# Float32r operands against pairs of float16 under powers of two, with transposing transfers that write the operand of p v, in a one-core attention and FFN block

## The reference

```
x = x + attn(layernorm(x))
    q = x wq, k = x wk, v = x wv                 (wq's first 128 of 192 columns of each head)
    probs = softmax(causal(q k^T * 192**-0.5))
    attn = concat_heads(probs v) wo
x = x + ffn(layernorm(x))
    h = relu(s0 * x W0) * 2 ; h = relu(s1 * scaled(h) W1) * 2 ; s2 * scaled(h) W2     (W: +1 or -1 from booleans)
```

## Time and profile before

| | |
|---|---|
| median of 3 executions | 1190.53 us (1190.52 to 1191.59) |
| the profiled execution's own time | 1192.84 us |
| its span, first to last instruction | 1191.0 us |
| PE busy | 1153.1 us, 97% |
| PE weight loads | 1007.5 us, 85% |
| ACT, DVE, POOL busy | 842.5, 835.0, 740.2 us |
| granted TensorE clock, mean | 0.987 |

### The profile page before, as it was taken

The page is one execution under the profiler, slowest core; times in us unless marked ns, Lnnn a source line. Parts: engine busy times, 40 slices in busy tenths (PEclk is TensorE's granted clock), DMA queues, the critical chain, the costliest instruction groups (busy, mean ns, idle before and its releaser), DMA issues.

```text
span 1191.0 us, 21994 instructions
## 1 busy us (share of the span) xinstructions
PE 1153.1 (97%) x6214; PEld 1007.5 (85%) x6214; DVE 835.0 (70%) x1560; ACT 842.5 (71%) x1447; POOL 740.2 (62%) x709
## 2 busy tenths in 40 slices
PE   6689999999999999999999999999999999999798
PEld 5578988888888988888898888888898888888577
DVE  6667676667777676677777776777767667677673
ACT  4477777777777776777777776777777677777653
POOL 2557666767757677677757676676766666773210
PEclk9889999999999999999999999999999999999899
DMA  4055553544455544444545454454554354444501
GB/s 133 14 107 109 109 109 82 119 94 86 97 108 110 109 100 90 98 107 88 106 103 112 91 110 95 82 115 93 108 110 103 84 117 99 86 107 74 109 1 71
DMA packets 354552, 114.36 MB, mean 96 GB/s; under 512 B 305888, under 2 KB 348384, under 8 KB 354528
## 3 DMA queue, kind: packets, MB, share of 16 engines
q1 hardware_dynamic: 354528, 114.08, 45.5%
HBM read 36.44 MB, written 2.10 MB: 32 GB/s over the span
## 4 chain that ended last, share of the span: by engine, by line
PE 94%; DVE 2%; issue 1%; ACT 1%; DMA 1%; POOL 0%; SPq 0%; DVEq 0%; ACTq 0%; POOLq 0%
PE psC L1012 59%; PE psS L1012 17%; PE psC L1137 17%; PE psS L1023 1%; DMA res<-in_L_attn_hidden_states 0%; DVE xn L803 0%; DMA pt<-p 0%; DVE psS L881 0%; ACT psS L656 0%; DVE res L904 0%; DVE p L889 0%; DVE xb L829 0%; POOL wqk L461 0%; ACT xb L627 0%; ACT p L668 0%
## 5 line engine op out<-in xcount | busy, mean ns | idle before, releaser
L1012 PE MATMUL psC<-xb,wqk 128*128 128x512 f32 x1350 | 343.6, 393 | 2.6 <-DVE xb L809 1.5
L881 DVE CUSTOM_DVE_ANT_0 psS<-psS,mask 128x128 f32<-128x128 f32 (+7 forms) x256 | 194.7, 766 | 161.9 <-PE psS L1012 161.9
L678 ACT ACTIVATE pT<-pt 128x256 fp32r<-128x256 f16 (+7 forms) x256 | 293.6, 1159 | 15.1 <-DMA pt<-p 14.9
L1012 PEld LDWEIGHTS psC<-xb,wqk 128*128 128x128 f32 x1350 | 249.2, 189 | 50.2 <-issue 3.5
L1012 PE MATMUL psS<-qkT 128*128 128x512 f32 (+2 forms) x1152 | 252.5, 347 | 12.5 <-DVE p L889 9.9
L656 ACT ACTIVATE psS<-psS,negmax 128x128 f32<-128x128 f32 (+7 forms) x256 | 182.9, 715 | 108.8 <-DVE negmax L881 106.7
L510 POOL TENSOR_TENSOR qkT<-qk,qkT 128x512 fp32r<-128x512 f32 x124 | 159.3, 1295 | 152.3 <-ACT qkT L647 152.3
L1012 PEld LDWEIGHTS psS<-qkT 128*128 128x128 f32 x1152 | 202.4, 192 | 43.1 <-DVE p L889 11.2
L1012 PE MATMUL psC<-wos,attn 128*128 128x512 f32 x768 | 217.2, 396 | 7.4 <-DVE attn L871 6.6
L1137 PE MATMUL psC<-pT,v 128*128 128x512 f32 (+2 forms) x1152 | 221.1, 346 | 0.0
L1137 PEld LDWEIGHTS psC<-pT,v 128*128 128x128 f32 x1152 | 196.6, 188 | 28.5 <-issue 0.4
(11 more groups left out here) (85 smaller groups left out, 870.8 us busy)
## 6 DMA issues: line engine op xcount, KB each, us to landing
raw<-in_L_attn_wkv SPq DMA_DIRECT2D x64, 256.0 KB, 3.7
raw<-in_L_attn_wq SPq DMA_DIRECT2D x32, 256.0 KB, 3.1
raw<-in_L_attn_wo SPq DMA_DIRECT2D x32, 256.0 KB, 2.8
pt<-p SPq DMA_TRANSPOSE x256, 3.4
res<-in_L_attn_hidden_states SPq DMA_DIRECT2D x8, 256.0 KB, 5.7
out<-res SPq DMA_DIRECT2D x8, 256.0 KB, 2.0
raw<-in_L_ffn_k SPq DMA_DIRECT2D x3, 256.0 KB, 3.7
scl<-in_L_ffn_s SPq DMA_DIRECT2D x3, 0.5 KB, 4.7
```

The source lines that it names most:

```text
L678: nc.scalar.activation(pT[:, :, places_of(n), :], src, ACT.Copy, scale=1.0 / UP).then_inc(placed, 1)
L881: nc.vector.tensor_tensor_reduce(row, row, mask[:, S - width:S], -SCALE, 3e38, ALU.add, ALU.min, negmax[:, n:n + 1]).then_inc(max_done, 1)
L1012: last = nc.tensor.matmul(out_ap, w, x, start=k == 0, stop=k == len(terms) - 1)
```

## The change

It does five things.

1. xb, wqk, wvs, qkT, v and pT become float16. A LO or HI of a weight or of x is then a float16. The layer norm's scale is multiplied by 2^9 (`X_UP`), and each head's q and k weights, and each pair's v weights, by a power of two that is made on the chip: ACT sums the squares of the rows of the loaded weights (`row_squares`, step `mx`), SP writes the 128 sums to DRAM (`put`) and reads them back to all partitions (`get`), DVE adds them up and takes the exponent by bit operations (`bounds`, step `sc`: five small instructions, four for v), and ACT multiplies the weights in place (`scale_weights`, step `r`). The scale comes off again in work that is there anyway: `OUT_DOWN` in the activations' scale and in what were tensor_tensor and are now scalar_tensor_tensor on DVE, `undo_qk` in the maxima, `undo_v` (step `rv`) at p v. The third split of the v weights takes one addition on POOL where it took two.
2. `h` and `l` write p16 with HI and LO blocks in turn, and the transposing transfer writes pT itself. `place` and the block of zeros are gone, and pT has a half for each parity of the head.
3. No stream is widened: scores of block 0 have 128 columns, block 4 is 512 and 128, the last diagonal block of p v is 128.
4. wo, attn and the FFN stay float32r; the FFN has its own buffers, and POOL's three waits for buffers before the FFN's weights go.
5. The orders, the preamble and the banks are new. The startup loads the first head's weights ahead of x and runs mx, put, get, sc and r before the first split.

The diff, cut to its core:

```diff
 TENSOR_ORDERS = ("""
-    pv1@-1 s3@0 v0@0 s4@0 v1@0 s5@0 x3@1 v2@0 x4@1 v3@0 s6@0 x5@1 o4@-1 s7@0 x6@1 o5@-1 x7@1 o6@-1 pv0@0 v4@0 o7@-1
-    s0@1 v5@0 s1@1 v6@0 o0@0 v7@0 o1@0 s2@1 o2@0 s3@1 o3@0 pv1@0 s4@1 x1@2 s5@1 x2@2 o4@0 x3@2 s6@1 x4@2 s7@1 x5@2
-    x6@2 o5@0 x7@2 o6@0 pv0@1 o7@0 x1@3 s0@2 x2@3 o0@1 o1@1 s1@2 o2@1 s2@2 o3@1""", """
+    pv1@-1 s2@0 v0@0 s3@0 v1@0 x1@1 s4@0 o4@-1 s5@0 v2@0 x2@1 v3@0 s6@0 x3@1 s7@0 x4@1 o5@-1 x5@1 o6@-1 x6@1 o7@-1
+    x7@1 v4@0 pv0@0 v5@0 s0@1 v6@0 o0@0 s1@1 v7@0 o1@0 s2@1 o2@0 s3@1 o3@0 pv1@0 s4@1 s5@1 x1@2 o4@0 x2@2 o5@0 s6@1
+    o6@0 x3@2 s7@1 x4@2 o7@0 x5@2 pv0@1 x6@2 x7@2 o0@1 o1@1 o2@1 o3@1 s0@2 s1@2""", """
...
 SCALAR_ORDERS = ("""
-    h5@-1 c3@-1 qk0@0 e6@-1 h6@-1 c4@-1 e7@-1 c5@-1 h7@-1 qk2@0 qk3@0 c6@-1 pv0@-1 qk1@0 snap0@1 e0@0 h0@0 c7@-1
...
+    e7@-1 h7@-1 pv0@-1 qk3@0 qk2@0 r0@1 e0@0 h0@0 e1@0 qk1@0 h1@0 mx0@2 pv1@-1 e2@0 v0@0 h2@0 e3@0 h3@0 v1@0 snap0@1
...
 SYNC_ORDERS = ("""
-    t7@-1 t0@0 t1@0 t2@0 lqk0@2 lo0@0 t3@0 t4@0 t5@0 t6@0 lv0@2 t7@0 t0@1 t1@1 t2@1 lo0@1 t3@1 t4@1 lqk0@3 lv1@2
-    t5@1 t6@1""", """
+    t1@-1 put0@1 t2@-1 t3@-1 get0@1 t4@-1 t5@-1 lqk0@2 t6@-1 t7@-1 t0@0 t1@0 t2@0 put0@2 t3@0 lo0@0 lqk0@3 t4@0
+    get0@2 lv0@2 t5@0 t6@0 put1@2 lo0@1 t7@0 get1@2 t0@1""", """
...
-        xb = sb("xb", [P, 7, 2, 2, CH], F32R)
-        v = sb("v", [P, 2, NT, GH * DN], F32R)
-        pT = sb("pT", [P, 2, PLACES, P], F32R)
+        v = sb("v", [P, 2, NT, GH * DN], F16)
...
+            def rows_to_dram(g, j, n):
...
+                    wait(sp, rows_max[0], g, 1, j, 1)
...
+                sp.dma_start(wmax_dram[at:at + 1, :].rearrange("a p -> p a"), wmax[:, at:at + 1]) \
+                    .then_inc(rows_out[n], 16)
...
+                sp.dma_start(wrow[:, at, :], wmax_dram[at, :].partition_broadcast(P)).then_inc(rows_in[n], 16)
...
-                            wait(sp, placed, g, 8, j, n - 1)
-                            sp.sem_inc(turn_go, 1)
-                        sp.dma_start_transpose(turned_blocks(n), p16[:, n % 2, 0:2 * (n + 1) * P]) \
+                        sp.dma_start_transpose(pT[:, j % 2, rows_of(n), :], p16[:, n % 2, 0:2 * (n + 1) * P]) \
                             .then_inc(turned[n % 2], 16)
...
+                nc.scalar.activation(src, src, ACT.Copy, scale=bound[:, at, 3:4]).then_inc(scaled[n], 1)
...
+                nc.scalar.activation(squares[:, :], src.rearrange("p a s -> p (a s)"), ACT.Square,
+                                     accum_out=wmax[:, at:at + 1]).then_inc(rows_max[n], 1)
...
-            def place(g, j, n):
-
...
-                src = turned_blocks(n).rearrange("p (w k) s -> p w k s", w=2)
-                nc.scalar.activation(pT[:, :, places_of(n), :], src, ACT.Copy, scale=1.0 / UP).then_inc(placed, 1)
...
-                nc.vector.tensor_tensor(to, product, base32, ALU.add).then_inc(gathered[n], 1)
+                nc.vector.scalar_tensor_tensor(to, product, OUT_DOWN, base32, ALU.mult, ALU.add).then_inc(gathered[n], 1)
...
+                width = (n + 1) * P
+                for a, b in [(0, min(width, CH)), (CH, width)][:1 + n // 4]:
...
-                wait(pe, placed, g, 8, j, 4 * c + 4)
+                for n in range(2):
+                    wait(pe, turned[n], g, 64, j, 32 * c + 32)
...
-                    o = psC[:, bank, (4 - max(n, 2)) * P:]
+                    n = 4 * c + 4 - i
+                    o = psC[:, bank, (i - 4 * c) * P:CH]
```

More of the change, by code:

```diff
@@ L12 @@
 U8 = mybir.dt.uint8
+U32 = mybir.dt.uint32
 P = 128
@@ L95, in exists @@
     h = GH * g + step[1]
-    if h == 0 and (step[0] in ("x", "a", "snap", "sum", "qk") or step[0] == "wv" and step[2] == 2):
+    if h == 0 and (step[0] in ("x", "a", "snap", "sum", "qk", "mx", "sc", "r", "put", "get", "lqk", "lv") or step[0] == "wv" and step[2] == 2):
         return False
@@ new lines, in load_values @@
+            def load_values(pair):
+                for c in range(2):
+                    sp.dma_start(raw[:, 5 + c, :].rearrange("p (c e) -> p c e", c=2),
+                                 wv_v[:, 2 * c:2 * c + 2, bass.ds(pair, 1), :].rearrange("p c a e -> p c (a e)")) \
+                        .then_inc(loaded["v"], 16)
+            def rows_to_dram(g, j, n):
+                at = 2 if n else j % 2
+                if n:
+                    wait_pair(sp, rows_max[1], g, 1, j, 1)
+                    sp.sem_inc(turn_go, 1)
+                    wait_pair(sp, rows_in[1], g, 16, j, 0)
+                else:
+                    wait(sp, rows_max[0], g, 1, j, 1)
+                    sp.sem_inc(turn_go, 1)
+                    wait(sp, rows_in[0], g, 16, j, -16)
+                sp.dma_start(wmax_dram[at:at + 1, :].rearrange("a p -> p a"), wmax[:, at:at + 1]) \
+                    .then_inc(rows_out[n], 16)
@@ L411, in sync_steps @@
                 for step, j, n in steps_of(SYNC_ORDERS, g):
-                    if isinstance(g, int) and GH * g + j == 0 and step in ("lqk", "lv"):
+                    if isinstance(g, int) and GH * g + j == 0 and step in ("lqk", "lv", "put", "get"):
                         continue
@@ L515, in split_out @@
                 wait(pool, done["o"], g, 8, j, 0)
-                split(raw[:, 2, :], wos[:, HI, :], wos[:, LO, :], wo_hi, wo_lo, lambda: wait(pool, wo_hi, g, 1, j, 1))
+                nc.gpsimd.tensor_tensor(wos[:, HI, :], raw[:, 4, :], one[:, :].to_broadcast([P, D]), ALU.mult) \
+                    .then_inc(wo_hi, 1)
+                wait(pool, wo_hi, g, 1, j, 1)
+                nc.gpsimd.tensor_tensor(wos[:, LO, :], raw[:, 4, :], wos[:, HI, :].bitcast(F32), ALU.subtract) \
+                    .then_inc(wo_lo, 1)
             def split_values(g, j, n):
@@ L650, in exponentials @@
             def exponentials(g, j, n):
-                width = (n + 1) * P
-                off = P if n == 4 else 0
                 wait(act, max_done, g, 8, j, n + 1)
-                row = psS[:, n % 2, off:off + width]
+                row = psS[:, n % 2, 0:(n + 1) * P]
                 nc.scalar.activation(row, row, ACT.Exp,
@@ L686, in pv_hi @@
                 wait(act, done["o"], g, 8, j, 4 * c)
-                nc.scalar.activation(attn[:, HI, :], psC[:, bank, :], ACT.Copy).then_inc(hi_done["pv"], 1)
+                if j % GH == 0 and c == 0:
+                    wait_pair(act, undo_ready, g, 1, j, 1)
+                nc.scalar.activation(attn[:, HI, :], psC[:, bank, :], ACT.Copy, scale=undo_v[:, :]) \
+                    .then_inc(hi_done["pv"], 1)
             def scalar_step(g, step, j, n):
@@ L921, in vector_step @@
                     sum_lo_part(n)
+                elif step == "sc":
+                    bounds(g, j, n)
+                elif step == "rv":
+                    undo_values(g, j)
                 elif step == "a":
@@ L944, in _ @@
                 norm_apply(t)
+            bounds(-1, 2, 0)
             dve.wait_ge(const_ready, 2)
@@ L1090, in scores @@
                 wait(pe, p_lo, g, 8, j, n - 1)
[L1091 to L1100 removed]
+                if isinstance(g, int) and GH * g + j == 0 and n < 2:
+                    pe.wait_ge(xt_lo, NT)
+                    pe.wait_ge(x32_done, NT)
+                width = (n + 1) * P
+                for a, b in [(0, min(width, CH)), (CH, width)][:1 + n // 4]:
+                    slot = qk_slot(j, K1 if a else K0)
+                    last = chain(psS[:, n % 2, a:b],
+                                 halves(lambda w: qkT[:, qk_slot(j, n // 4), w, n % 4 * P:(n % 4 + 1) * P],
+                                        lambda w: qkT[:, slot, w, 0:b - a]))
                 last.then_inc(done["s"], 1)
```

370 lines of the change are left out of this document (200 added, 170 removed).

## The result

The kernel after takes 1296.55 us (median of 4 runs, 1292.82 to 1298.54) against 1190.53 for the kernel before: a ratio of 1.089 (95% interval 1.086 to 1.091), 106 us slower. The forecast was 1121 us with a range to 1180, and 0.06 for slower.

What follows compares the result with a forecast made beforehand. PE bounds the loop: columns plus a fixed charge per matmul. Columns -15.4, charge -58.6, seam +4.5, start +4, end -4 make -69.5 us: 1192.8 to 1123.3 profiled, 1121 as median; own range 1106 to 1134, whole range 1098 to 1180.

Steps and rivals of the forecast that it cites:

- the scale's chain: Loop's mx, put, get, sc, r: two transfers of about 3.5 us and 4 us of small work, hidden, 0 us.
- The slower rival: Transposes into pT blocks 1 KB apart land late, holding h and pv1; slower from about 8.2 us landing; chance 0.05.
- The columns: PE's scores and p v: nine matmuls a head go from 256 to 128 columns, 15.4 us off.
- the rival with a floor of 104 ns: PE's 128 column float16 matmuls last 104 ns, giving back 18.3 us, so 1139 us; chance 0.12.
- The charge: PE's fixed cost per matmul with its weights: 14.3 ns falls to 3 ns for 5190 float16 matmuls, 58.6 us off.
- The rival that the charge stays: PE's float16 matmuls keep the charge: 1180 us, or 1151 with half left; chances 0.14 and 0.08.
- The seam: Between rounds, PE waits at s0 for POOL's LO of the next K: 0.3 us a round, 4.5 us in all.
- the rival in which the chain from s7 to pv1 runs out by 1 to 2.5 us a round: lqk's 512 KB before t6 and t7 delay pv1: 15 to 38 us, so 1136 to 1158; chance 0.12.
- The engines' loads: In the loop, ACT, DVE and POOL stay below the new 63.1 us round: 38.7, 52.6 and 45.3 us; 0 us.
- The ends: Start, with its scale round trips, net +4 us; end, with pv1 starting earlier, -4 us.
- The charge's bounds: PE's float16 matmuls: 0 to 5 ns of charge left in the forecast's own range, around the 3 ns taken.
- the ends' bounds: Start between -5 and +10 us around +4; end between 0 and -6 us around -4.

Runs made afterwards that it cites:

- e3: Changed kernel with the loop's puts written to DRAM with words 4 KB apart, get reading old sums; 1146.19 us, 0.962 of before.
- e5: Changed kernel with the loop's puts written to DRAM with words 64 bytes apart, get reading old sums; 1144.13 us.
- e10: Kernel before plus three unread puts of 128 words a round on SP, words 64 bytes apart; 1191.65 us, 1.000 of before.
- e4: Kernel before plus three unread puts of 128 words a round on SP, side by side in DRAM; 1448.48 us, 1.216 of before.
- e1: Changed kernel without put, get and their waits after the first pair, later heads using the first heads' sums; 1147.48 us, 0.963 of before.
- p2: Changed kernel with all sums over partitions by a ones matmul, no put or get, DVE's first bounds moved earlier; 1140.47 us, 0.957 of before.
- p1: Changed kernel with the sum over partitions by a ones matmul on PE after the first pair; 1153.80 us, 0.970 of before.
- e6: Changed kernel with all puts, still side by side, issued from ACT's queue instead of SP's; 1247.67 us, from runs of 1234.06 and 1261.28.
- e8: Changed kernel with the loop's puts cut to 32 words side by side, get still reading 128; 1153.32 us, ratio 0.965 to 0.970 to before.

## Why the prediction was wrong

**The step that failed** is the scale's chain, priced as "two transfers of about 3.5 us ... hidden, 0 us". Its 3.5 us were the landing of loads of 256 KB and of transposes; before has no write of 4-byte words to DRAM, and this transfer needed a bound from above that no row gave. It landed in 6.9 us and more. The step did see that SP's waits for put and get can hold the transposes behind them, then `h` and pv; it took two transposes between put and get for cover enough, and priced a late one at "one landing, 3.5 us". These waits came to 30.8 us of SP in the loop. What it left out is that a put in flight holds other transfers with no wait for it: a transpose takes SP 9 us to issue where it takes 1.3, then `h`, `l` and `s` wait. The reader of `get` was hidden well enough: DVE's two waits for it, 16.7 us in all, are at the start. e3 and e5 against after, and e10 against e4, show it: with the same number of transfers, 150 and 257 us depend on where the words land.

**The slower rival** had the right path and the wrong cause. It said that late transposes hold `h`, then PE, and that it decides from a landing of some 8.2 us. In after those behind a put occupy SP alone for up to 9.95. But it laid the lateness to the pieces 1 KB apart, which e1 refutes (landing 3.3). Because that cause looked improbable, the path got 0.05.

**The columns**, -15.4 us, held as far as rows tell. PE's timeline of e1 shows six x matmuls, twelve of v and three of s0:

```profile
207.21 1.46 PE L1111 MATMUL psC<-xb,wqk 128*128 128x512 f16 x6
208.51 1.46 PE L1111 MATMUL psS<-qkT 128*128 128x512 f16 x6
...
220.06 1.47 PE L1111 MATMUL psC<-wvs,xb 128*128 128x256 f16 x12
221.37 0.33 PE L1111 MATMUL psS<-qkT 128*128 128x128 f16 x3
221.53 1.47 PE L1111 MATMUL psC<-wvs,xb 128*128 128x256 f16 x12
222.76 0.94 PE L1111 MATMUL psC<-wos,attn 128*128 128x512 f32 x3
```

Three of 128 columns take 221.53 - 221.37 = 0.16 us, 53 to 55 ns each, which is their columns: the rival with a floor of 104 ns is refuted. (A float16 chain in front of a float32r one can't be read this way: 222.76 - 221.53 is 1.23 us for twelve of 256, less than their 1.28 us of columns, and the float32r chain then shows as much too long. Only chains with float16 behind them are used.)

**The charge**, -58.6 us, went as forecast and was a little too large. Chains go from 1.37 to 1.30 us for six of 512 (208.51 - 207.21; 3.3 ns over the columns each) and from 1.43 to 1.31 for twelve of 256 (221.37 - 220.06; 2.5 over). Over a whole round it is more: 147,456 columns are 61.44 us, 0.43 us are the two short waits at the seam and at pv1, and of the 2.2 us left 48 float32r matmuls would take 0.7 at 14.3 ns each; 324 float16 ones have 4.7 ns each. That is 0.6 us a round over the forecast, some 9 us in all. The rival that the charge stays is refuted. The weight loads got shorter too, in the costliest groups of after:

```profile
L1104 PEld LDWEIGHTS psC<-wos,attn 128*128 128x128 f32 x768 | 147.0, 198 | 51.6 <-issue 9.4
...
L1104 PEld LDWEIGHTS psC<-wvs,xb 128*128 128x128 f16 x1536 | 150.2, 99 | 29.4 <-issue 0.3
```

A float16 load is recorded at 99 ns, a float32r one at 198 (190 in e1). In before all loads are of 4 bytes, 1007.5 us of them. That the charge is what a 4-byte load can't hide remains a reading of these rows and is not shown; no run here separates load from stream.

The Trainium skill, "TensorE: Matmul & The Clock Gate", section "Wait — 56ns, not 53.3ns?", gives 2.5 ns over the columns; the single chains agree (2.5 and 3.3), three of 128 columns are at 0 to 2, the round as a whole is at 4.7. The Trainium skill, same page, section "Back-to-back issue gap", would have 81 ns for 128 columns; s0 disagrees, with 53 to 55.

**The seam**, 0.3 us a round, held once the puts are gone. The two waits of e1's round, on PE's timeline:

```profile
189.46 0.67 PE L1111 MATMUL psS<-qkT 128*128 128x128 f16 x6 [0.23 <-POOL qkT L547]
190.33 4.38 PE L1222 MATMUL psC<-pT,v 128*128 128x512 f16 x24 [0.20 <-issue]
```

The first is the wait for POOL's LO as forecast. The second, at pv1, is 0.20 us, so the rival in which the chain from s7 to pv1 runs out by 1 to 2.5 us a round is refuted.

**The engines' loads** were right: ACT 682.7 us for 660, DVE 887.9 for 900, and neither sets a round. POOL writes a LO as float16 in 1159 ns where it took about 1290.

**The ends.** The end's -4 is -5.7 in after and -6.1 in e1. The start's +4 was too small by much: +30.9 in after and +15.5 in e1, whose three startup puts land in 7.6 us and gets in 5.3, where 3.5 was taken for each. Without them p2's first pv1 is at 86.47, only 1.3 us behind before's, 12.3 ahead of p1's and 14.2 ahead of e1's. So of the 31 us, 12 to 14 are the startup's own round trips and about 15 the loop's puts in the first pair.

**The balance.** e1 has the sum of the prediction without its failed step: +15.5 - 55.6 - 6.1 = -46.1 us of span, where -69.5 was forecast. Of the 23.4 between them 11.5 are the start, 9.3 the rounds, nearly all of it the charge, and 4.5 what the first and the last pair save, which the sum held beside the ends and the measured stretches hold in them; the end gives 2 back. The failed step is the 149 us between e1 and after.

**The ranges.** The charge's bounds alone (0 to 5 ns) give 1105 to 1131 us, and with the ends' bounds 1094 to 1141; the stated 1106 to 1134, and 1098 as the low end of the whole range, don't follow from them. After lies outside all of these.

**Still open:** why writes that lie close in DRAM are slow, whether it counts how many share a stretch or how many engines meet in it, and how they hold transfers that go elsewhere. e6 says only that a shared queue isn't needed for it.

## What to carry to other kernels

Price a new transfer by a row of its own form, pieces, size and spacing, and when there is none, treat its landing as unknown from above; then ask not only who waits for it but what is issued behind it and who waits for that. A value in each partition shouldn't be written side by side to DRAM next to transfers with a deadline: words 16 bytes apart took the landing from 6.9 us and more to 1.6 here, and a matmul with ones did away with the round trip, for 0.5 us a round. When a rival's path is real, its chance shouldn't hang on the one cause that came to mind for it.

## What the runs showed of the hardware that was not expected

- In the loop, 128 words of 4 bytes to DRAM land in 6.9 us or more side by side, 3.3 at 8 bytes apart, 1.6 at 16, 1.5 at 64 and at 4 KB, 1.7 in SBUF. 48 such puts of 512 bytes cost 257 us in e4, and nothing in e10.
- Such a put holds others. Over all of after a piece of a transfer took its engine 16 x 1296.8 us x 0.555 / 368,352 = 31.3 ns on average, against 24.2 in e1 (16 x 1144.9 x 0.470 / 355,392), by the rows of the queue:

```profile
q1 hardware_dynamic: 368352, 117.25, 55.5%
```

```profile
q1 hardware_dynamic: 355392, 114.28, 47.0%
```

The trace's records of single pieces, taken by size, say which got longer. The 4-byte pieces, the puts' among them, did not: they average 9.0 ns in after and 9.2 in e3. The pieces of 2048 bytes did (419 ns in after, 105 in e3; the longest 7.7 us against 0.9), and the pieces of 256 bytes a little (23.5 against 21.4). A slow put is thus seen in the late landing and in its neighbours, not in the records of its own pieces.

- Slack ends abruptly: from e8, with a put of 5.6 us, to after, with 6.9 and more, the steady round goes from 64.1 to 71.2 to 76.2 us.
- A float16 matmul with its weights costs 0 to 2 ns over its columns at 128 columns, 2.5 at 256 and 3.3 at 512, each read from a single chain, where a float32r one costs 12.5 to 15.
